# Attention's last eleven steps: scores in a ring of five PSUM banks instead of three

## The reference, cut to what matters

```python
h = _modulate(_ln(x), sh_msa, sc_msa)
qkv = (h @ w_qkv + b_qkv).reshape(B, N, 3, nh, hd).transpose(2, 0, 3, 1, 4)
attn = softmax(einsum('bhqd,bhkd->bhqk', q, k) * hd ** -0.5, axis=-1)
o = einsum('bhqk,bhkd->bhqd', attn, v).transpose(0, 2, 1, 3).reshape(B, N, C)
x = x + g_msa[:, None, :] * (o @ w_proj + b_proj)
xn = _modulate(_ln(x), sh_mlp, sc_mlp)
# gate, top 2 of 4 experts, gelu MLP of 288 -> 1152 -> 288 per expert
return x + g_mlp[:, None, :] * moe
```

## Time and profile before

| what | value |
|---|---|
| three runs | 932.76, 937.58, 937.92 us; median 937.58 |
| the profiled execution | 935.8 us |
| its span | 934.1 us |
| mean granted TensorE clock in it | 0.941 |
| attention's tail, step 5 to V(15), in it | about 484 to 517 us |

### The profile page before, as it was taken

One profiled execution on the slowest core, in us unless ns is written; L12 is line 12 of the kernel. 1 busy time (PEld: TensorE's weight loads), 2 busy tenths in 40 slices (PEclk: granted clock), 3 DMA queues, 4 the chain that ended last, 5 costly groups with the idle time before them and its releaser, 6 DMA issues. The chain is left out here.

```text
span 934.1 us, 15252 instructions
## 1 busy us (share of the span) xinstructions
PE 829.1 (89%) x5111; PEld 555.0 (59%) x5111; DVE 569.0 (61%) x994; ACT 476.3 (51%) x975; POOL 339.3 (36%) x339
## 2 busy tenths in 40 slices
PE   4897799999999999999988885279999999999995
PEld 3693333433334333433322563179999999999995
DVE  3776778777787778778860494725545434434432
ACT  0451277677676777677777364344434333333331
POOL 6544321131202222110832077166546434434432
PEclk9897599999999999999999795589999999999998
DMA  8011401324131221303212495153332222222221
GB/s 222 11 54 33 87 2 24 78 89 93 22 78 36 48 60 23 71 12 85 78 52 70 116 290 160 52 144 87 69 62 38 42 43 46 34 43 45 35 34 20
DMA packets 56129, 62.73 MB, mean 67 GB/s; under 512 B 24056, under 2 KB 50534, under 8 KB 55480
## 3 DMA queue, kind: packets, MB, share of 16 engines
q1 hardware_dynamic: 46580, 47.27, 19.3%
q0 software_dynamic: 8400, 12.12, 7.9%
q10 hardware_dynamic: 1076, 2.36, 1.0%
HBM read 33.61 MB, written 15.46 MB: 53 GB/s over the span
## 5 line engine op out<-in xcount | busy, mean ns | idle before, releaser
L1074 DVE TENSOR_REDUCE negmax<-m_ps 128x2 f32<-128x1024 f32 x256 | 306.6, 1221 | 70.5 <-PE m_ps L1143 69.9
L1042 ACT ACTIVATE probs<-s_ps 128x512 f32<-128x512 f32 x512 | 269.8, 602 | 105.8 <-PE s_ps L1176 105.8
L1176 PE MATMUL s_ps<-stack 56*128 56x512 f32 x512 | 161.0, 478 | 20.3 <-ACT probs L1042 19.6
L1176 PEld LDWEIGHTS s_ps<-stack 56*128 56x128 f32 x512 | 65.3, 185 | 180.6 <-ACT probs L1042 152.1
L1143 PE MATMUL m_ps<-stack 54*128 54x512 f32 x512 | 136.7, 453 | 9.8 <-DVE negmax L1074 4.6
L1190 PE MATMUL o_ps<-probs,v_aug 128*19 128x512 f32 x1024 | 135.8, 602 | 6.3 <-ACT o_sb L1049 5.1
L2017 PE MATMUL gate_bank<-weights,ht_hi 128*128 x630 | 127.1, 296 | 0.4 <-DVE ht_lo L1913 0.4
L1993 PE MATMUL h_ps<-weights,xt_hi 128*128 x525 | 115.1, 350 | 5.2 <-DVE xt_hi L1906 5.2
L1003 POOL CAST parts<-proj_f 128x512 fp32r<-128x512 f32 x28 | 17.1, 610 | 257.0 <-ACT proj_f L1034 133.4
L1691 POOL DMA_INDIRECT out<-res,ido x35 | 56.9, 1627 | 140.7 <-DVE res L1935 140.7
L1739 ACT CAST ht_hi<-ht_ps 128x384 fp32r<-128x384 f32 x105 | 43.5, 488 | 119.6 <-PE ht_ps L2004 119.6
(11 more groups left out here) (214 smaller groups left out, 1119.7 us busy)
## 6 DMA issues: line engine op xcount, KB each, us to landing
stack<-parts SPq DMA_DIRECT2D x84, 144.0 KB
w_raw<-in_L_cond_w SPq DMA_DIRECT2D x9, 432.0 KB, 3.5
w_raw<-in_L_cond_w SPq DMA_DIRECT2D x9, 384.0 KB, 3.7
xn_scratch<-h SPq DMA_DIRECT2D x16, 192.0 KB, 4.1
x_in<-in_x SPq DMA_DIRECT2D x4, 576.0 KB, 9.4
o_scratch<-o_norm SPq DMA_DIRECT2D x16, 144.0 KB, 2.4
o_in<-o_scratch SPq DMA_DIRECT2D x16, 144.0 KB, 2.5
xr<-in_x SPq DMA_DIRECT2D x16, 144.0 KB, 3.1
```

The costliest lines, as they stand in the source:

```text
L1042: nc.scalar.activation(probs[:, st % 2, h], s_ps[k % S_BANKS][:], ACT.Exp, scale=SCALE)\
L1074: nc.vector.tensor_reduce(negmax[:, half, first:first + count], m_ps[n % 2][:], AX.X, ALU.max, negate=True)\
L1176: nc.tensor.matmul(s_ps[k % S_BANKS][:], stack[s][r, j, 1, kt // QT, (kt % QT) * P:(kt % QT + 1) * P], stack[s][r, j, 0, half], start=True ...
```

## The change

From step 5 of the last group on (`plan.tail`, item 496), score items go round five banks: the three of before, in the order in which they come free, and the second bank of each of the two `m_ps` tiles. The first three items of the tail wait as before. From the fourth on, an item waits for the exponential of five items before instead of three, and for VectorE's last reduction of maxima (`plan.last_max`, item 284). ScalarE reads the same bank by `score_bank`. In these steps TensorE's order is: scores of pair 0, scores of pair 1, the step's item if there is one, V(st - 1). All other steps stay as they are.

```diff
--- before.py
+++ after.py
@@ -808,6 +808,7 @@
 BLOCKS = 2 * GH * QT
 PAIR_BLOCKS = 2
 S_BANKS = 3
+TAIL_BANKS = S_BANKS + 2
 AHEAD = 44
 RATE = 4
 PROJ_AT = (1, 4, 7, 10)
@@ -848,6 +849,9 @@
             self.maxima(items, AHEAD + RATE * (t + 1))
             due = range(begun, self.block // BLOCKS)
         self.turn(self.last, "out", 2 * GG - 1)
+        tail = next(t for t in reversed(range(len(self.steps))) if any(it[1] == "max" for it in self.steps[t])) + 1
+        self.tail = score_item(tail // STEPS, tail % STEPS, 0)
+        self.last_max = max(it[0] for items in self.steps for it in items if it[1] == "max")
 
     def maxima(self, items, upto):
         while self.block < min(upto, 2 * GG * BLOCKS):
@@ -909,6 +913,12 @@
         def max_bank(n):
 
             return m_ps[n % 2][:, 0]
+
+        def score_bank(k):
+
+            spare = [m_ps[i][:, 1] for i in range(2)]
+            first = [s_ps[(plan.tail + i) % S_BANKS][:] for i in range(S_BANKS)]
+            return s_ps[k % S_BANKS][:] if k < plan.tail else (first + spare)[(k - plan.tail) % TAIL_BANKS]
 
         block = ctx.enter_context(nc.Block())
 
@@ -1039,7 +1049,7 @@
                 act.wait_ge(slot_mm, k + 1)
                 if h == 0:
                     act.wait_ge(pv_free, 16 * g + st + 1)
-                nc.scalar.activation(probs[:, st % 2, h], s_ps[k % S_BANKS][:], ACT.Exp, scale=SCALE)\
+                nc.scalar.activation(probs[:, st % 2, h], score_bank(k), ACT.Exp, scale=SCALE)\
                   .then_inc(slot_free, 1)
 
             def out_of_bank(turn):
@@ -1171,9 +1181,13 @@
                     pe.wait_ge(rows_ld[half][j], 64 * (g + 1))
                 for hh in range(2):
                     k = score_item(g, st, 2 * j + hh)
-                    pe.wait_ge(slot_free, k + 1)
+                    if k < plan.tail + S_BANKS:
+                        pe.wait_ge(slot_free, k + 1)
+                    else:
+                        pe.wait_ge(slot_free, k + 1 - (TAIL_BANKS - S_BANKS))
+                        pe.wait_ge(max_free, 2 + plan.last_max + 1)
                     r = slice(hh * heads.BLOCK, hh * heads.BLOCK + heads.MAX_ROW + 2)
-                    nc.tensor.matmul(s_ps[k % S_BANKS][:], stack[s][r, j, 1, kt // QT, (kt % QT) * P:(kt % QT + 1) * P],
+                    nc.tensor.matmul(score_bank(k), stack[s][r, j, 1, kt // QT, (kt % QT) * P:(kt % QT + 1) * P],
                                      stack[s][r, j, 0, half], start=True, stop=True).then_inc(slot_mm, 1)
 
             def values(g, st):
@@ -1199,14 +1213,18 @@
             for g in range(GG):
                 for st in range(STEPS):
                     items = plan.steps[STEPS * g + st]
+                    tail = score_item(g, st, 0) >= plan.tail
                     scores(g, st, 0)
+                    if tail:
+                        scores(g, st, 1)
                     for it in items[:1]:
                         item(*it)
                     if st >= 1:
                         values(g, st - 1)
                     elif g >= 1:
                         values(g - 1, STEPS - 1)
-                    scores(g, st, 1)
+                    if not tail:
+                        scores(g, st, 1)
                     for it in items[1:2]:
                         item(*it)
                     unit = PROJ_AT.index(st) if st in PROJ_AT and g + 2 < GG else None
```

## The result

The changed kernel takes 924.73 us (median of 6 runs, 922.99 to 929.3), the kernel before 936.24 us (6 runs, 932.56 to 937.92). The ratio is 0.9889, with a 95% interval from 0.9859 to 0.9919: 1.1% faster, 10.4 us (11.5 us between the medians), where I had forecast 0.8% and 7.9 us. Part of that is the base: I subtracted from 937.58, the median of three runs, and with six it is 936.24.

A forecast was written before the change was run, and what follows sets the result against it. Banks, V and latency were taken to set the tail's 2.655 us step, with ScalarE the bound at 1.95 us after the change. A gain of 7.9 us from 937.58 gave 929.7 us, range 925.5 to 935.5.

The forecast's parts named there:

- What bounds the tail: Tail steps: banks, V and latency set 2.655 us a step; with enough banks ScalarE bounds at 1.95 us.
- Entry: Step 5: the first spare-bank score waits for the last reduction, moving V(4) by 0.05 us, to 485.95.
- Step 8: New stall: pair 1's score waits for row maxima until 492.4, V(7) at 492.8, costing some 1.3 us of gain.
- Pace of the exponentials: ScalarE in the tail: exponentials in an unbroken line start 0.487 us apart.
- Second wait: Scores from item 499 on: an added wait on VectorE's count, taken as 0.05 us each, hidden behind ScalarE.
- rival 2: Tail: TensorE becomes the bound at 2.31 us a step; gain 5.7 us, time 931.9 us; chance 0.15.
- The sum: Whole kernel: the tail's 7.9 us gain taken from the median 937.58 gives 929.7 us, 0.8% faster.
- Behind attention: After V(15): copy, transposes, division and barrier stay the same, so the whole 7.9 us passes through.
- rival 3: Output projection: the clock falls differently and helps, 4.3 us less at full clock, 925.4 us; chance 0.10.
- Rival 4: Output projection: clock stays at half, 1.36 us more per tile, up to 17.4 us and 947 us; chance 0.05.
- Rival 5: Steps 5 to 8 gain nothing through late spare banks or row maxima; gain 4.9 us, 932.7 us; chance 0.10.
- The chances: Whole kernel: faster by over 1% 0.25, slower by over 1% 0.02, within 1% 0.73.

The follow-up runs named there:

- two queues: Changed kernel with the four last row-maxima transfers of pair 1 issued by GpSimd instead of on SyncE's queue; 925.19 us, ratio 0.9858.
- one wait: Changed kernel with the wait on VectorE's last reduction only ahead of the first two items in spare banks; 925.52 us, ratio 0.9863.
- The filler: Kernel before, with matmuls that nobody reads added in TensorE's idle time of the tail; 932.77 us, ratio 0.9941.

## Why the prediction was right, and where it fell short

**What bounds the tail: right.** Banks, V and latency set the step; ScalarE sets it now. The experiments add that a step gets to ScalarE's pace only by both halves of the change, which I had not said: the order alone gives 2.6 of the 7.3 us, 1.6 of them in the last step, and the banks alone give none.

**Entry: nearly right.** V(5) and V(6) came as forecast, to 0.01 us behind V(4). The new wait cost nothing, but the new order did: V(4) lost 0.18 us where I gave it 0.05.

**Step 8: right place, size off.** I let the score start with the last packet in the DMA slices, 0.8 us behind the end of the issue. The run shows 1.09 us, and the earlier trace rows had 1.08. The nearer row was the one with the same waiter, not the one with the packets: between a packet and the matmul that waits for it lie another 0.3 us (in the changed run the last small packets end by 489.7 and the score starts at 489.98). With this V(7) comes 0.37 us later than forecast. I put the cost of the stall at 1.3 us of the gain; two queues bring V(7) forward by 1.63 us, of which 0.96 are left at V(15).

**Pace of the exponentials: right within 0.003 us.** It is 0.490 us from end to end against 0.487. The Trainium skill ("ScalarE: Activation LUTs", section "What ACT_TABLE_LOAD costs") has figures that make 612 - 93 = 519 ns for 512 columns, an estimate; the trace differs and decides, for 490.

**Second wait, rival 2: fell.** V to V is 1.96 us with it and without, not 2.31.

**The sum.** From V(4) to V(15) the forecast gains 7.94 us (30.29 - 22.35), the run 7.33. Of the 0.61 between them 0.37 arise up to V(7), 0.16 up to V(9), and the rest behind it. With the loss at the entry the tail gave 7.15 against 7.9. This would have made the changed kernel slower than forecast, and it came out 5 us faster: 1.3 us of that is the base of three runs, the rest is the next point.

**Behind attention: this step failed.** "I pass the whole 7.9 us through" put the change of TensorE's clock at nothing. It took for granted that an execution of the kernel before has the tail of the one profile that I had, at a granted clock of 1.00. It need not: the second profile shows 5.6 us of half clock's cost in the same tail. So the change is worth 7.2 to 7.6 us where the clock stays up, and the runs gained about 4 more by the clock, 104 us at half clock instead of 117. That the time came out where rival 3 had it (925.4) is in part luck: rival 3 put the whole help of the clock into the output projection, 4.3 us on top of the 7.9 and with no half-clock stretch left there. The stretch was still there, 6.9 us in the first profile of the changed kernel and 13.7 in that with one wait.

The filler shows that idle time in the tail is a place from which the time at half clock can be lowered: nothing else was changed there, and that gave 102 us instead of 117, as many as the changed kernel has. What is not shown is in which part of the executions the kernel before falls in its tail, since only two of its executions were traced, nor in which stages the changed kernel saves its 13 us. Idle time as a sum does not order the versions either. From V(4) to V(15) TensorE is idle for 6.3 us in the kernel before, 4.4 with the order alone, 2.6 in the changed kernel; but with the banks alone it is idle for 9.2 us before the clock falls, and that version has 111 us at half clock, not more than the kernel before. So why the order alone already has only 103 stays open.

**Rival 4** did not happen. Rival 5 neither: the row maxima arrived at about the time that it names (6.73 us behind V(4)), but V(8) came 2.1 us earlier than before, where the rival had no gain.

**The chances.** I had given 0.25 to a kernel faster by more than 1%. It is 1.1% faster, with an interval of 0.8 to 1.4%.

## What to carry to other kernels

In this loop of two engines and a ring of buffers, more buffers helped only when the order of the issuing engine let them fill before the long piece of work. Try buffers and order apart before you credit either.

In this kernel TensorE's idle gaps cost time through its clock as well as through the waits. One profile tells the clock of one execution: work out the time at half clock for all runs before a term is taken from one trace.

For a wait on small transfers take the time from the end of their issue to the waiter's start from a row with the same waiter.

## What the runs showed of the hardware that I had not expected

TensorE's granted clock fell from 1.00 to 0.50 in the middle of the tail, although no gap between its matmuls was longer than 0.6 us ahead of the fall (0.57 at the turn of the half, 0.45 in the other steps). The row of 483.0 to 496.3 in the second profile of the kernel before has TensorE busy for 10.50 of 13.30 us, with the clock at 1.00, and the fall came at its end. In another execution of the same program, with 10.57 of 13.40 us, it did not fall. At 12.83 of 13.40, with the filler, it did not either (one profile). The Trainium skill ("TensorE: Matmul & The Clock Gate", Part 1) says that the clock follows TensorE's past activity and at another phase in each run; the traces agree, with a fall at 496.3 in one profile of the kernel before and none before 520.6 in the other. Eleven matmuls that nobody reads went with a granted clock of 1.00 through the end of a block in one profile, and the matmuls behind them ran at full clock from the first.
